# Attention and an 8-bit feed-forward on one core: loads reordered, down chunks padded to 128 rows, gate weights scaled by GpSimd, peaks spread by transposes

## The reference

```python
def attend(x, ctx):                      # x: layernorm(x), ctx: 4 x 256 x 128
    query, key = ctx @ Wq.T + bq, ctx @ Wk.T + bk
    attention = softmax(query @ key.T)   # 256 x 256 per batch
    return x @ attention.T

def ffn(x):                              # x: layernorm(x), 1024 x 256; hidden size 704
    qx, sx, sc = reorder_quantize(x, up_index)        # rows scaled to 448, rounded to fp8
    g = qlinear(qx, sx, sc, w_gate)[:, down_index]
    u = qlinear(qx, sx, sc, w_up)[:, down_index]      # weights scaled by row peaks, rounded to fp8
    qt, st, sct = reorder_quantize(silu(g) * u, down_index)
    return qlinear(qt, st, sct, w_down)
```

## Time and profile before

| | us |
|---|---|
| median of 3 runs | 79.10 (79.03 to 79.25) |
| the profiled execution's own time | 79.58 |
| its span (first to last event of the engines) | 77.8 |
| busy in the span: PE, DVE, ACT, POOL | 69.9, 61.1, 56.9, 49.0 |

### The profile page before, as it was taken

One profiled execution on the slowest core, in us unless ns is written; L12 is line 12 of the kernel. 1 busy time (PEld: TensorE's weight loads), 2 busy tenths in 40 slices (PEclk: granted clock), 3 DMA queues, 4 the chain that ended last, 5 costly groups with the idle time before them and its releaser, 6 DMA issues.

```text
span 77.8 us, 1587 instructions
## 1 busy us (share of the span) xinstructions
PE 69.9 (90%) x520; PEld 57.6 (74%) x520; DVE 61.1 (79%) x159; ACT 56.9 (73%) x118; POOL 49.0 (63%) x78
## 2 busy tenths in 40 slices
PE   4999999799959999999999999996989979998940
PEld 4999548589938988999887997984765746676710
DVE  1059899899995999988599999808999999992060
ACT  6106899997899889896899997996288371695400
POOL 5103135369649055987989887899998975853330
PEclk9999999999999999999999999999999999999999
DMA  0999899910000000000000011210240101042204
GB/s 13 272 414 418 258 366 412 409 53 8 0 4 4 0 0 0 0 0 8 0 0 0 34 38 34 67 24 1 85 118 0 67 0 56 11 135 71 70 6 135
DMA packets 4088, 6.98 MB, mean 90 GB/s; under 512 B 656, under 2 KB 2448, under 8 KB 4080
## 3 DMA queue, kind: packets, MB, share of 16 engines
q1 hardware_dynamic: 3888, 6.53, 23.5%
q0 software_dynamic: 192, 0.36, 1.4%
HBM read 5.48 MB, written 1.41 MB: 89 GB/s over the span
## 4 chain that ended last, share of the span: by engine, by line
PE 47%; POOL 22%; ACT 12%; issue 9%; DVE 7%; POOLq 0%; DVEq 0%; ACTq 0%
PE gate_ps L1258 9%; POOL act_g L402 9%; POOL wd_scatter L335 8%; PE tT_ps L1086 7%; PE gate_ps L1162 3%; PE up_ps L1137 3%; PE bank_s L1241 3%; PE tT_ps L1209 3%; PE tT_ps L1073 3%; ACT act_g L591 2%; DVE grid_t L769 2%; PE bank_s L1185 2%; DVE y_sb L892 2%; POOL qxT_bf L395 2%; ACT kT L495 2%
## 5 line engine op out<-in xcount | busy, mean ns | idle before, releaser
L402 POOL TENSOR_TENSOR act_g<-act_g,up_scale 128x704 f32<-128x704 f32 x8 | 13.6, 1695 | 1.1 <-ACT act_g L591 1.0
L1162 PE MATMUL gate_ps<-w_hi,qxT 128*128 128x352 f32 x32 | 11.0, 345 | 0.3 <-ACT act_g L591 0.3
L1209 PE MATMUL tT_ps<-ident,sum_t 128*128 128x128 f32 x48 | 10.4, 283 | 0.3 <-ACT tT L613 0.2
L383 POOL TENSOR_TENSOR sum_w<-sum_w,grid_w 128x256 f32<-128x256 f32 x6 | 4.1, 683 | 10.2 <-DVE sum_w L772 10.2
L1162 PE MATMUL gate_ps<-w_lo,qxT 128*128 128x352 f32 x32 | 10.2, 322 | 0.0
L414 POOL TENSOR_TENSOR x_sb<-y_sb,x 128x256 f32<-128x256 f32 x7 | 6.6, 945 | 5.6 <-DVE y_sb L892 5.6
L857 DVE TENSOR_TENSOR t_sb<-up_ps,act_g 128x704 f32<-128x704 f32 x8 | 7.1, 885 | 3.6 <-POOL act_g L402 2.2
L1212 PE MATMUL tT_ps<-negidentb,grid_t 128*128 128x128 bf16 x48 | 9.6, 219 | 0.0
L613 ACT ACTIVATE tT<-tT_ps 128x768 bf16<-128x768 f32 x7 | 5.7, 808 | 4.9 <-PE tT_ps L1212 4.7
L1086 PE MATMUL tT_ps<-attT,xT 128*128 128x256 f32 x32 | 7.6, 381 | 0.9 <-issue 0.9
L548 ACT ACTIVATE grid_w<-wup_sb,s_w 128x256 bf16<-128x256 f32 x12 | 5.2, 497 | 4.3 <-DVE s_w L808 4.3
(11 more groups left out here) (117 smaller groups left out, 203.6 us busy)
## 6 DMA issues: line engine op xcount, KB each, us to landing
wup_sb<-w_gate_up_dram SPq DMA_DIRECT2D x3, 512.0 KB, 4.8
x_sb<-x_dram SPq DMA_DIRECT2D x4, 256.0 KB, 8.0
xT<-x_t_dram SPq DMA_DIRECT2D x2, 512.0 KB, 9.6
out_dram<-x_sb SPq DMA_DIRECT2D x8, 128.0 KB, 1.7
wdn_sb<-w_down_dram SPq DMA_DIRECT2D x1, 704.0 KB, 6.6
head_sb<-head_dram SPq DMA_DIRECT2D x1, 416.0 KB, 5.4
wdnT<-wd_scatter SPq DMA_DIRECT2D x6, 64.0 KB, 1.9
ctx_sb<-ctx_t_dram SPq DMA_DIRECT2D x1, 256.0 KB, 6.8
```

The source lines that it names most:

```text
L402: nc.gpsimd.tensor_tensor(act_g[:, i % NT], act_g[:, i % NT], up_scale[:, :], ALU.mult)\
L1162: last = nc.tensor.matmul(ps[:, h, 0:IH], qxT[:, b, c, j * P:(j + 1) * P].bitcast(F32R), w[:, c, a, h * IH:(h + 1) * IH].bitcast(F32R), st ...
L1209: nc.tensor.matmul(to, sum_t[:, i % NT, of], ident[:, :], start=True, stop=False, is_transpose=True)
```

## The change

- SP issues head second, then x of batch 0, ctx, the second pair of up weights, the down weights, the index, x of batches 3, 1 and 2, the third pair, and the two xT loads.
- WARM_UP is 9 in place of 24.
- The last down chunk: only its 64 fresh rows are loaded back, the other 64 partitions are cleared by POOL once among the constants, and down multiplies over all 128 partitions.
- diag_up and its buffer are gone. scale_up on POOL multiplies the gate part of chunk k (128x256) by the row peaks after subtract_up, and turn_up transposes the result by the identity.
- spread and spread_up use the transpose mode.
- Tile 7 is moved from SCALED_BY_ACT to SUMMED.
- All four hand-written orders are new. On POOL the scatters begin ahead of scale_act(0). On DVE residual(3), bn_stats2(3), peak_of_x(2) and peak_of_x(3) come ahead of hidden(0). On PE turn_t(2) and gates(7) come behind down(0).

```diff
-WARM_UP = 24
-SCALED_BY_ACT = (0, 3, 6, 7)
-SUMMED = (1, 2, 4, 5)
+WARM_UP = 9
+SCALED_BY_ACT = (0, 3, 6)
+SUMMED = (1, 2, 4, 5, 7)
...
-                sp.dma_start(wdnT[:, k], wd_dram[chunk(k), :]).then_inc(wdnT_in, 16)
+                sp.dma_start(wdnT[P - fresh[k]:, k], wd_dram[P * k:P * k + fresh[k], :]).then_inc(wdnT_in, 16)
...
             load_up(0)
+            load_head()
+            load_x(0)
+            load_ctx()
             load_up(1)
-            load_head()
             load_down()
-            load_ctx()
+            load_idx()
+            load_x(3)
             load_x(1)
             load_x(2)
-            load_x(0)
             load_up(2)
-            load_idx()
             load_xT(0)
-            load_x(3)
             load_xT(1)
...
                 nc.gpsimd.tensor_copy(identb[:, :], ident[:, :])
+                nc.gpsimd.memset(wdnT[0:P - fresh[KC - 1], KC - 1], 0.0)
...
-                nc.gpsimd.tensor_tensor(q_w[:, k, 0], sum_w[:, k, 0], grid_w[:, k, 0], ALU.subtract).then_inc(q_w_done, 1)
-
-            def diag_up(k):
-                if k == 0:
-                    after("ident")
+                step(nc.gpsimd.tensor_tensor(q_w[:, k, 0], sum_w[:, k, 0], grid_w[:, k, 0], ALU.subtract), ("q_w", k))
+
+            def scale_up(k):
+                after(("q_w", k))
                 pool.wait_ge(peak_w_done, k // 2 + 1)
-                nc.gpsimd.tensor_scalar(diag_w[:, k, 0], ident[:, :], peak_w[:, k, 0:1], 1.0, ALU.mult, ALU.mult)\
-                    .then_inc(diag_w_done, 1)
+                nc.gpsimd.tensor_scalar(q_w[:, k, 0], q_w[:, k, 0], peak_w[:, k, 0:1], 1.0, ALU.mult, ALU.mult)\
+                    .then_inc(q_w_done, 1)
...
-                            nc.tensor.matmul(wuT_ps[k % 2][:, c, a], q_w[:, k, a, c * P:(c + 1) * P],
-                                             diag_w[:, k, a], start=True, stop=True)
+                            nc.tensor.transpose(wuT_ps[k % 2][:, c, a], q_w[:, k, a, c * P:(c + 1) * P], ident[:, :])
...
-                                            start=True, stop=True)
+                                            start=True, stop=True, is_transpose=True)
...
-                                            peak_w[:, k, 1:2].to_broadcast([P, P]), ident[:, :], start=True, stop=True)
+                                            peak_w[:, k, 1:2].to_broadcast([P, P]), ident[:, :], start=True, stop=True,
+                                            is_transpose=True)
...
-                    last = nc.tensor.matmul(y_ps[i], tT[P - fresh[k]:, i % 2, k], wdnT[P - fresh[k]:, k],
+                    last = nc.tensor.matmul(y_ps[i], tT[:, i % 2, k], wdnT[:, k],
                                             start=(k == 0), stop=(k == KC - 1))
```

More of the change, by code:

```diff
@@ L904, in _ @@
             scales_up(0)
+            bn_stats1(0)
+            grids_up(0)
+            bn_aggr1(0)
+            sums_up(0)
             peak_of_up(1)
-            grids_up(0)
+            score_max(0)
+            grids_up(1)
             reciprocal_up(1)
+            peak_of_down()
+            reciprocal_of_z(0)
             scales_up(1)
-            grids_up(1)
-            sums_up(0)
+            sums_up(1)
+            score_max(1)
+            bn_stats1(1)
             grids_up(2)
-            peak_of_down()
@@ L931, in _ @@
+            reciprocal_of_z(1)
+            bn_stats1(2)
+            sums_up(2)
+            reciprocal_down()
             reciprocal_up(2)
+            residual(0)
             grids_up(3)
             reciprocal_of_z(2)
+            scales_down()
+            scales_up(2)
+            split_up(0)
             grid_down(0)
-            scales_up(2)
-            residual(0)
+            score_max(3)
             sums_up(3)
             bn_stats2(0)
+            split_up(1)
+            grids_up(4)
@@ L964, in _ @@
             grids_x(1)
-            grid_down(1)
-            sum_down(1)
-            bn_stats2(2)
-            bn_aggr2(2)
+            residual(3)
+            bn_stats2(3)
+            bn_aggr2(3)
+            peak_of_x(2)
+            reciprocal_x(2)
+            scales_x(2)
+            peak_of_x(3)
             hidden(0)
             peak_of_t(0)
-            peak_of_x(2)
+            grids_x(2)
             reciprocal_t(0)
-            reciprocal_x(2)
-            scales_x(2)
+            scales_t(0)
@@ L975, in _ @@
+            reciprocal_x(3)
             hidden(1)
-            scales_t(0)
             peak_of_t(1)
-            residual(3)
             grid_of_t(0)
-            grids_x(2)
+            scales_x(3)
             reciprocal_t(1)
-            bn_stats2(3)
             scales_t(1)
+            grid_of_t(1)
             hidden(2)
-            bn_aggr2(3)
-            grid_of_t(1)
+            sum_of_t(1)
+            grids_x(3)
             peak_of_t(2)
-            peak_of_x(3)
             reciprocal_t(2)
-            sum_of_t(1)
@@ L991, in _ @@
-            reciprocal_x(3)
+            hidden(3)
             scales_t(2)
-            grid_of_t(2)
-            scales_x(3)
-            sum_of_t(2)
-            grids_x(3)
-            hidden(3)
             peak_of_t(3)
             reciprocal_t(3)
+            grid_of_t(2)
+            scales_t(3)
             hidden(4)
             peak_of_t(4)
-            scales_t(3)
+            sum_of_t(2)
+            hidden(5)
             reciprocal_t(4)
             grid_of_t(3)
-            hidden(5)
+            scale_y(0)
@@ L1028, in _ @@
             grid_of_t(7)
+            sum_of_t(7)
             scale_y(5)
@@ L1293, in _ @@
             ups(0)
-            turn_down(1, 0)
             gates(2)
-            turn_down(1, 1)
             ups(1)
-            attend(3)
+            turn_x(2)
+            gates(3)
             ups(2)
-            gates(3)
-            turn_x(2)
             turn_t(0)
             gates(4)
+            turn_x(3)
             ups(3)
+            gates(5)
+            ups(4)
             turn_t(1)
-            gates(5)
-            turn_x(3)
-            turn_t(2)
-            ups(4)
             gates(6)
             ups(5)
+            down(0)
+            turn_t(2)
             gates(7)
-            down(0)
-            ups(6)
             down(1)
             turn_t(3)
-            ups(7)
+            ups(6)
             down(2)
             turn_t(4)
+            ups(7)
             down(3)
```

240 lines of the change are left out of this document (114 added, 126 removed).

## The result

The changed kernel takes 84.03 us (82.83 to 85.09, four runs) against 79.17 (79.03 to 79.27, four runs) for the kernel before beside it: ratio 1.0537, 95% interval 1.0407 to 1.0666. The forecast was 77.9, faster; the kernel is slower, beyond the range's end of 80.1. Every ratio here leaves out the runs that lie more than 1.5% above the fastest of their kernel (the four differ mainly in the granted clock, 0.974 to 0.994), so this one rests on 82.83 and 83.99 us, and where too few runs are left none is given. The profiled execution is the longest run, 85.09 us; its span is 82.3, and those of the four are 80.5 to 82.3. It lies 2.8 us above its span, the kernel before 1.78: of the 5.5 us between the two profiled executions 4.5 are span, and for the other 1.0 no row gives a cause.

The account below looks back on a forecast made before the run. DVE bounds the front to hidden(0), then POOL's scatters and scale_act, then DVE and PE alternate. down(0) 57.1, turn_t(7) 70.65, plus 5.96: span 76.6 against 77.8, so median 79.1 - 1.2 = 77.9 us (chance 0.43), range 76.3 to 80.1.

Parts of the forecast that it names:

- the path behind down(0): From down(0) at 57.1 us, PE reaches turn_t(7) at 70.65, with DVE through at 70.5, so moving tile 7 costs nothing.
- among the transposes: Rival, chance 0.03: PE's clock falls during turn_up, turn_att, turn_x and turn_down in front; 82.4 us.
- The first rival: Chance 0.19: the load back doesn't end last; DVE sets the end, turn_t(7) near 69.3 us, time 76.6.
- The head at 5.56 us: Start of the first projection on PE, forecast at 5.85 us in place of 8.14, 2.3 us earlier.
- the last scatter: End of scatter(5) on POOL, forecast at 49.6 us against 50.88 before.
- the last 6 us: From turn_t(7) to the end of the span: 6.3 less 0.34 for six fewer bf16 products, 5.96 us.
- the work taken from PE: New PE instructions save 3.3 us; 3.0 of it hides under DVE's 29.91 us in front and gains nothing.
- down(0) within 0.8: Start of down(0) on PE, forecast at 57.1 us against 58.45, with PE waiting for the load back.
- Nothing of the reordered loads is late by these numbers: Front: x(0) lands near 6.4 us, the second up pair near 8.3, where DVE reaches peak_of_up(1) at 8.7.
- The low clock at head: Rival, chance 0.24: PE stops for 1.9 us after warming, first products run slower, score_max(0) about 12.1; 80.1 us.
- Given back on POOL: Rival, chance 0.11: POOL's dense 15.2 us stretch by 1.2, or DVE's front waits a microsecond more; 79.1 us.
- the reading of the microsecond from 31 in the earlier trace: 13 PE instructions start there, nearly all transposes, at full pace: taken as evidence against the clock falling during transposes.

Follow-up runs that it names:

- experiment 9: Changed kernel with ten products of zeros on PE ahead of down(2): 82.68 us, ratio to the kernel before 1.0402.
- experiment 2: Changed kernel with scale_act over 88 of its 704 columns, the rest left unscaled: 78.05 us, ratio 0.9738, span 76.8.
- experiment 5: All new instructions of the change, but with the old orders, old loads and 24 warming products: 80.0 us, ratio 1.0008 to the kernel before.
- experiment 7: Kernel before with 9 warming products: 79.7 us, ratio 0.9965; also all new instructions, old orders, new loads, 24 warming products: 81.88 us, ratio 1.0232.
- experiment 11: Changed kernel with each scale_act as two instructions of 352 columns, same values: 86.66 us, no ratio.

## Why the prediction was wrong

The step that failed is the one on the path behind down(0): "DVE, which now makes sum_of_t(7) too, is through at 70.5". It took DVE's instructions at their length alone and costed the holds at nothing; sum_of_t(7) ends at 75.74. The rows for it were there: I had 2.0 us of excess in the eight grids of the kernel before, and grid_of_t(5) at 1.44 us beside scale_act(7), but used them as an argument against a rival and not as a term of the sum. The term should have been worked out for the new order, by laying POOL's scale_act calls over DVE's list.

- *The size of that term.* 4.9 us of excess in the tail's grids, where the kernel before had 2.0, and 2.0 us at s_x(2) ahead of hidden(0), where s_x(2) in the kernel before is not held. With short scale_act calls the span is 76.8, beside the 76.6 forecast.
- *Its consequence.* PE idled 2.15 us before down(2) and its clock fell, worth up to 1.8 us (experiment 9). The forecast had a fall at the front (0.24) and among the transposes (0.03), and none in the tail.
- *The path by numbers.* hidden(3) to turn_t(7) takes 76.25 - 52.24 = 24.0 us in place of 71.50 - 52.70 = 18.8: 5.2 more. On DVE that is 2.9 of holds and 2.4 of work moved into the stretch, with the idle time unchanged; the slower clock is no term beside these, it shows there as 0.61 us of waiting for ups(7). The first rival's own sum says the same: 14.1 us from hidden(4) to the end of grid_of_t(7), where 18.4 were measured (56.31 to 74.75), with 3.1 of holds and 1.0 of waits. With short scale_act calls (experiment 2) hidden(3) to turn_t(7) takes 18.0.
- *What was right.* The head at 5.56 us, the last scatter within 0.8, the last 6 us within 0.1, and that the work taken from PE would be hidden (experiment 5; 3.6 us in place of 3.3). down(0) within 0.8 is luck: it was released by ups(5), not by the load. Moving head did start the first half earlier. hidden(0), though, came at 42.17 against 38.5: 2.0 us from s_x(2), and 2.7 of waits where the forecast had 0.8, the longest 1.5 for x(0). It didn't reach hidden(3), which scale_act(3) released.
- *The loads.* "Nothing of the reordered loads is late by these numbers" did not hold: DVE waited 1.50 us for x(0), and the second pair landed near 9.5 us, not 8.3. In the new order the pair cost no wait; in the old one it costs 3.6 us, so loads and orders stand or fall together.
- *Rivals.* The first one's condition came true: down(0) did not wait for the load back, and DVE set the end. Its gain went into the holds, which it named as the thing against it. The low clock at head gave 80.1 and would have had the sign right, but its condition did not: PE stopped for 0.29 us and not 1.9, and project_k(0) took 1.41 us to the next start in place of 0.86; experiment 7 shows a slower start free in the kernel before. "Given back on POOL" had the wrong direction: POOL took 15.3 us from scatter(0) to the end of the last (15.2 forecast), DVE's work beside it was stretched. No fall of the clock among the transposes was seen (1.00 from 4.50 to 42.17 us). But the reading of the microsecond from 31 in the earlier trace rows was wrong: of the ten instructions that start there three are in transpose mode, the others are products by the diagonal and bf16 products, so it said nothing against that rival.

The Trainium skill, page "GPSIMD Engine Reference", section 1, says that the shared interface causes contention with DVE instructions that run in a two-port mode or have two SBUF inputs. The measurements agree on both: the plain grid, with 0.40 us for 704 columns against 0.88 for hidden, is of the first kind, and sum_of_t and the grid with the constant tile are of the second. They also agree on those that aren't held: peak_of_t (one input), hidden (one input in PSUM), single columns. I had cited the page for its first half alone. The page gives no size; here it is the whole rest of POOL's instruction.

## What to carry to other kernels

Before you change an order by hand, lay the long POOL instructions over DVE's list, and give each DVE instruction of the two kinds the full rest of the POOL instruction that it meets: the profile books it as busy time, and the clearest sign is a row longer than its fellows. A mean that differs from the shortest of its group (640 against 390 ns here) is a price that depends on timing, so any change that shifts one engine against the other, even one that only takes work away, redeals it. Put reductions, PSUM reads and single columns beside the long POOL instructions, and don't expect to free DVE by cutting those into pieces that follow one another without a gap (pieces with a gap were not tried).

## What the runs showed of the hardware

- The hold can outlast one POOL instruction: 3.56 us through two scale_act calls, 4.74 through six instructions, for work of 0.4 and 0.15. It does not always: s_x(2) came free at the end of scale_act(0), though the next two of POOL's followed as closely as in experiment 11. What decides it stays open. What DVE had to do was done afterwards: 0.2 us between the end of scale_act and that of a plain grid, 0.75 for the sum.
- It goes both ways: yscale_of beside sum_of_t(2) takes 0.83 us (58.18 to 59.01, the sum ends at 58.96), where it takes 0.19 alone, and add_residual takes 1.37 and 1.44 beside two sums in the kernel before, where it takes 0.72 to 0.82 elsewhere. The one that began first ran at its usual length.
- s_x(2) starts 0.42 us before scale_act(0), long enough for its 0.15, and was held all the same, with scatter(2) in POOL's row until then (38.85 to 39.89). grid_of_t beside scatter(3) was not held (0.40). Which of POOL's steps begins the hold stays open.
- Two elements per partition were held and one was not: 2.15 us for s_x(2) against 0.21 for its two single columns, and s_t, a single column, takes 0.14 inside scale_act(4).
- The granted clock's column reads 1.00 while the first projection of experiment 7 runs at half pace (2.08 us for two products against 1.02); the pace of equal instructions is the surer sign at the start of a kernel.
